# One instruction per tile in place of one per pair of tiles for VectorE's product of gathered rows with silu'd gates

## The reference

```python
dk = jax.nn.silu(edge_attr @ Wdk.T + bdk)
dv = jax.nn.silu(edge_attr @ Wdv.T + bdv)
q_i = q[dst]
k_j = k[src]
v_j = v[src]
attn = jnp.sum(q_i * k_j * dk, axis=1)
attn = jax.nn.silu(attn) * _cosine_cutoff(edge_weight)
msg = v_j * dv * attn[:, None]
agg = jax.ops.segment_sum(msg, dst, num_segments=x.shape[0])
out = agg @ Wo.T + bo
return x + out
```

## Time and profile before

| what | value |
|---|---|
| median of 3 runs | 2825.9 us |
| the profiled execution | 2828.56 us |
| its span, first to last instruction | 2826.3 us |
| PE busy | 2354.1 us (83%) |
| DVE busy | 2156.4 us (76%) |
| POOL busy | 2136.9 us (76%) |
| ACT busy | 1938.9 us (69%) |
| granted TensorE clock, mean | 0.949 |

### The profile page before, as it was taken

One profiled execution on the slowest core, in us unless ns is written; L12 is line 12 of the kernel. 1 busy time (PEld: TensorE's weight loads), 2 busy tenths in 40 slices (PEclk: granted clock), 3 DMA queues, 4 the chain that ended last, 5 costly groups with the idle time before them and its releaser, 6 DMA issues. The chain is left out here.

```text
span 2826.3 us, 52157 instructions
## 1 busy us (share of the span) xinstructions
PE 2354.1 (83%) x12012; PEld 1904.9 (67%) x12012; DVE 2156.4 (76%) x6159; ACT 1938.9 (69%) x4051; POOL 2136.9 (76%) x1792
## 2 busy tenths in 40 slices
PE   7497888888888888888888888888888888888878
PEld 5254676676777676767676776766777767766666
DVE  4586878777878777787777787777777777777776
ACT  3474777777777677777777776777777777767766
POOL 1675878778787788777878778888877778777862
PEclk9799899999999999999999999999999999999999
DMA  8786777877888777788778778778877777778765
GB/s 237 198 215 242 211 234 229 238 234 227 235 236 230 228 224 227 226 234 237 227 231 232 228 234 237 233 229 232 234 231 229 233 231 229 224 234 233 223 188 182
DMA packets 321332, 642.50 MB, mean 227 GB/s; under 512 B 83932, under 2 KB 141648, under 8 KB 321304
## 3 DMA queue, kind: packets, MB, share of 16 engines
q0 software_dynamic: 129840, 418.60, 52.3%
q1 hardware_dynamic: 191464, 223.60, 25.7%
HBM read 583.26 MB, written 58.74 MB: 227 GB/s over the span
## 5 line engine op out<-in xcount | busy, mean ns | idle before, releaser
L949 POOL DMA_INDIRECT e_kv<-kv_tab,e_idx x1568 | 1959.3, 1250 | 495.4 <-issue 453.7
L1153 DVE TENSOR_TENSOR e_gated<-e_kv,e_gate 128x1024 f32<-128x1024 f32 x788 | 954.7, 1221 | 506.5 <-DMA e_kv<-kv_tab,e_idx 504.2
L1081 ACT ACTIVATE e_gate<-e_gate_ps 128x1024 f32<-128x1024 f32 x786 | 780.9, 1020 | 234.2 <-DVE e_gated L1153 217.1
L1097 ACT ACTIVATE weighed_hot<-hot,e_attn 128x128 f32<-128x128 bf16 x1580 | 520.4, 401 | 365.6 <-DVE e_attn L1172 353.9
L1000 PE MATMUL e_sum_ps<-e_gated,weighed_hot 128*128 128x256 f32 x3168 | 750.8, 380 | 3.9 <-ACT weighed_hot L1097 3.9
L1012 PE MATMUL e_gate_ps<-wd_hi_lo,high 128*128 128x512 f32 x1572 | 677.2, 431 | 13.5 <-issue 13.5
L1000 PEld LDWEIGHTS e_sum_ps<-e_gated,weighed_hot 128*128 128x128 f32 x3168 | 603.6, 191 | 101.2 <-ACT weighed_hot L1097 4.7
L1013 PE MATMUL e_gate_ps<-wd_bias,low 128*128 128x512 f32 x1572 | 650.3, 414 | 0.0
L1162 DVE CUSTOM_DVE_ANT_0 e_gated<-e_gated,e_q_ps 128x256 f32<-128x256 f32 x1576 | 573.9, 415 | 0.7 <-PE e_q_ps L1032 0.7
L1031 PE MATMUL e_q_ps<-q_win,hot_t 128*128 128x256 f32 x1572 | 465.1, 323 | 47.7 <-DVE e_dot L1162 47.4
L1020 PE MATMUL e_hot_ps<-ident_bf,hot 128*128 128x128 bf16 x1568 | 160.3, 226 | 315.6 <-DVE hot L1179 315.4
(11 more groups left out here) (156 smaller groups left out, 1398.7 us busy)
## 6 DMA issues: line engine op xcount, KB each, us to landing
e_attr<-attr_groups_dram SPq DMA_DIRECT2D x784, 128.0 KB, 4.6
e_q_next<-q_tab SPq DMA_DIRECT2D x98, 256.0 KB
e_kv<-kv_tab,e_idx POOLq DMA_INDIRECT x1568, 4.5
sum_tab<-e_sums SPq DMA_DIRECT2D x100, 128.0 KB, 4.3
e_prior<-sum_tab SPq DMA_DIRECT2D x99, 128.0 KB
kv_tab<-l_kv_out SPq DMA_DIRECT2D x49, 256.0 KB, 3.5
q_tab<-l_q_out SPq DMA_DIRECT2D x49, 256.0 KB, 3.2
sum_tab<-zeros SPq DMA_DIRECT2D x25, 256.0 KB, 2.9
```

The source lines that it names most:

```text
L949: pool.indirect_dma_start(kv[:, k, :], None, kv_tab, bass.IndirectOffsetOnAxis(ap=idx[:, k:k + 1], axis=0)).then_inc(kv_landed[k // G][k % ...
L1081: nc.scalar.activation(gate[:, 2 * p:2 * p + 2, :], gate_ps[:, 2 * p:2 * p + 2, :], ACT.Silu).then_inc(silu_ready[s][p], 1)
L1097: last = nc.scalar.activation(weighed_hot[:, s % 2, k, :], hot[:, s, :, k], ACT.Copy, scale=attn[:, s * G + k:s * G + k + 1])
L1153: nc.vector.tensor_tensor(gated[:, pair(s, p), :], kv[:, pair(s, p), :], gate[:, 2 * p:2 * p + 2, :], ALU.mult).then_inc(gated_ready[s][p], 1)
```

## The change

`gate_rows` issues one product per tile, 128x512, in place of one per pair, 128x1024. The waits ahead of the first and the signal behind the last stay what they were; between the two stands no wait. A step has 16 such products in place of 8. Nothing else is changed.

```diff
                     dve.wait_ge(kv_landed[s][p], visit.now32 if c >= 2 else visit.late32)
                     dve.wait_ge(silu_ready[s][p], visit.of(c, 2))
-                    nc.vector.tensor_tensor(gated[:, pair(s, p), :], kv[:, pair(s, p), :], gate[:, 2 * p:2 * p + 2, :],
-                                            ALU.mult).then_inc(gated_ready[s][p], 1)
+                    for k in (2 * p, 2 * p + 1):
+                        last = nc.vector.tensor_tensor(gated[:, s * G + k, :], kv[:, s * G + k, :], gate[:, k, :], ALU.mult)
+                    last.then_inc(gated_ready[s][p], 1)
```

## The result

| | median | runs | from, to |
|---|---|---|---|
| before | 2833.47 us | 4 | 2824.22 to 2845.34 |
| changed | 2577.02 us | 4 | 2565.35 to 2578.25 |

The ratio is 0.9084, 95% interval 0.9034 to 0.9133: the changed kernel is 9.2% faster, some 256 us.

A forecast was written before the change was run, and what follows sets the result against it. GpSimd's gathers, delayed by VectorE's products, were taken as the bound. Terms of -86 and +14 us gave -72, from 2828.6 to 2756.6, less 2.7 for the runs' median: 2754 us, range 2670 to 2850.

The forecast's parts named there:

- What bounds the kernel: Edge stage: GpSimd's row of 1568 gathers sets the pace, 25.05 us a step, with 474 us of delays.
- VectorE's extra time costs nothing: Split products add 55 us on VectorE, covered by its 504 us of waiting for rows; chance of its showing 0.05.
- Halves let a plain gather through: A gather meeting just one product goes on at the boundary between its halves; -86 us over 448 gathers.
- The replay: 448 gathers delayed by one product, replayed at their old places against halves: -97, -7 and +18, sum -86 us.
- the slower rival: Halves without a wait block gathers as one product: 47 us slower, 2873 us; 0.20 together with more chained delays.
- The failed step: Gathers kept from an earlier instruction over one or two products stay kept over halves: 86 and 60 gathers, +14 us.
- The chained delays: Gathers arriving as a short instruction gives way to a product without a gap wait it out: 146 gathers, 255 us.
- The 5 in 63: At boundaries between two whole products without a gap, already kept gathers got through 5 times in 63.
- 8 of 8 behind a gap of 0.03 us: Already kept gathers got through 8 of 8 times where 0.03 us or more lay open between whole products.
- The lower bound: Every kept gather is let through at the first half: 86 x 0.61 + 60 x 1.75 = 157 us gained.
- Phases spread: Rival: gathers fall anywhere against VectorE's products, so halves gain 143 us, 2683 us; chance 0.14.
- Phases move: Rival: gathers shift against VectorE, 41 more chained delays swallow the 72 us, 2798 to 2854 us; chance 0.13.

The follow-up runs named there:

- e7: Kernel before with only the second pair of each group (p = 1) split into two products: 2762.7 us, ratio 0.9717.
- e6: Kernel before with only the first pair of each group (p = 0) split into two products: 2672.02 us, ratio 0.9422.
- e18: Kernel before, whole products, with VectorE waiting for its own preceding instruction only ahead of each group's first product: 2608.31 us, ratio 0.922.
- e16: Kernel before, whole products, with VectorE waiting for its own preceding instruction ahead of every product: 2531.29 us, ratio 0.8936.
- e17: Changed kernel (halves) with VectorE waiting for its own preceding instruction only ahead of each group's first product: 2534.74 us, ratio 0.8956.
- e1: Kernel before with the whole product's operands written as one run of 1024 elements: 3199.94 us, ratio 1.0021 (before 3192.31).
- e3: Kernel before with the attention ahead of the attributes' subtraction instead of behind it: 3109.54 us, ratio 0.9745 (before 3192.31).
- e11: Kernel before with three tiny memsets on VectorE ahead of the loop: 3241.8 us, ratio 1.0008 (before 3244.08).
- e12: Changed kernel with three tiny memsets on VectorE ahead of the loop: 3230.93 us, ratio 0.9953 (before 3244.08).
- e10: Changed kernel with an already fulfilled wait ahead of each half: 3311.74 us, ratio 1.0177 (before 3244.08).
- e8: Changed kernel with each tile's product cut once more, four products of 256 columns per pair: 2750.15 us, ratio 0.9689.
- e4: Kernel before without the gates, the product becoming gathered rows times 1.0 with one SBUF input: 3161.98 us, ratio 0.9919.

## Why the prediction was wrong

**What bounds the kernel: right.** In every run where the kernel before took some 2830 us, time follows the gathers' delays nearly one to one: 474 us and a span of 2826 before, 423 and 2778 (e7), 319 and 2663 (e6), 255 and 2601 (e18), 223 and 2574 (changed), 152 and 2529 (e16). The last point has lost a tenth: delays fell by 322 and the span by 297, and of the missing 25 us GpSimd's idle time before its gathers has 23 (518 where it was 495).

**VectorE's extra time costs nothing: right.** The halves take 683 ns, as the subtraction's row had it, and VectorE's busy time in the stage rose from 1923 to 1966 us where 55 were added. Its wait for rows fell to 212 us; 377 had been forecast on the smaller gain, and 504 less 252 less 55 is 197.

**Halves let a plain gather through: right; the size in part by luck.** The replay said 86 us, 94 were measured. But the replay kept every gather at its place and left some 430 of the 448 delayed, and 334 were: others arrive there now. Where a gather met a half in progress with another half right behind it, it went on between the two in 210 of 231 cases; the slower rival, that halves without a wait block as one, is out.

**The failed step: "I take it that they hold such a gather as the whole did: 86 x 0.07 + 60 x 0.14 = +14 us".** The chained delays fell by 197 us. With what was measured the sum comes out: -94 - 197 + 38 (gathers now let in at the ends of the subtraction, the attention and the sums) = -253 against the measured 252. The 5 in 63 on which it rested counted boundaries between two products, for gathers that had been kept already. But the halves do their work one boundary earlier, ahead of the first product: at the end of the attention, where the kernel before kept 75 of 76 and the changed kernel lets in 55 of 70, and at the end of the sums, where the kernel before kept 46 of 57 and the changed kernel lets in 68 of 77. And 8 of 8 behind a gap of 0.03 us, which stood in the same sentence, was the better lead: e16, e17 and e18 are built on it and no gather was kept. The lower bound that the prediction named for this term, 157 us, was called far off; 197 exceed it, since the bound let a gather go at the first half and not ahead of it. (Some 20 us of the 38 that came back are these same places, at the ends of the attention and of the sums; net of them, 177.)

**The rivals.** "Phases spread" had the direction and 143 us, by another road: the plain delays gained little more than the replay. "Phases move" had seen that half of the delay hangs on 0.05 us and that it "could as well lose them", but put no price and no chance on that side.

**What stays open.** Why a product of 512 behind the attention leaves the boundary open when 1024 and 256 don't, with VectorE's instructions at the same distances from the gather, and why 256 delays nobody behind the sums. Neither the operands' form (e1), nor the 4-column instruction (e3), nor the place in the stream (e11, e12), nor an added wait (e10) explains it. That a gap opens it is shown; what happens at a boundary without one is not. Open too is what bounds the groups at 3200 us. There the mean granted TensorE clock was 0.86 to 0.90 in place of 0.94 to 0.98, and GpSimd stood idle 721 to 1272 us before its gathers in place of 490 to 519. 39 to 159 of these waits lasted over 3 us, where the other groups have at most one, and nearly all fell ahead of a gather of even number, where the program waits for VectorE's products. VectorE in turn stood still for up to 10.9 us at a time in e11, against 3.6 in the kernel before. The lower clock goes with it; that it is the cause isn't shown. The same kernels that gain 9 to 11% elsewhere end within 2% of the kernel before.

## What to carry to other kernels

When an instruction on one engine takes several times its median, lay it beside the other engine's timeline and sort it by what ended when it went on: the kinds have different remedies, and the rare long ones can be worth more than the many short ones (here 146 gathers of 1568 held 255 of the 474 us of delays). If GpSimd issues gathers and sets the pace, and VectorE runs instructions with two SBUF inputs back to back, look first for gathers kept over several of them; let VectorE wait for its own last instruction ahead of the first long one (0.21 us four times a step bought 223 us here), and only then cut the long ones. Don't cut for its own sake: halves gained 9%, quarters 3%, and halves on top of the four gaps another 74 us. Such a gain lasts only while the gathers are the bound: with another bound the same change was worth 0.5% (e12).

## What the runs showed of the hardware

- An indirect DMA's issue on GpSimd, which reads its indices from SBUF, waits out a VectorE product with two SBUF inputs that is in progress 0.13 us after its start, for 1.07 us of a 1024-element product or 0.53 us of a 512-element one. SBUF — State Buffer of the Trainium skill, § Who interferes with whom, has the rule (a VectorE instruction with two SBUF inputs contends with a GpSimd instruction that reads SBUF); the trace agrees. The same section says of a probe that tensor_tensor did not stall a DMA; this one, with its indices in SBUF, it does stall. The longest such gather took 1.98 us behind whole products (e18) and 1.47 behind halves (e17).
- A boundary between two VectorE instructions without a gap does not always let a waiting gather in. One was kept 3.1 us in e8, through ten of them; behind a gap of 0.13 us none of 93 was (e16).
- The sums (one input in PSUM, one in SBUF) delayed none of 90 gathers with a gap behind them (e16), kept 46 of 57 with a 1024-element product right behind them (before), held 68 of 77 to their own end with a 512-element one (changed), and delayed none of 21 with a 256-element one (e8).
- The fixed part of this VectorE product between two starts was 0.07 us at 256, 512 and 1024 elements (0.34, 0.60 and 1.14 us from start to start, 1.04 ns an element), against some 0.15 us in the recorded durations (0.42, 0.68 and 1.22 us).
- A float tensor_scalar from SBUF to SBUF took 701 ns for 1024 elements, even when written with a step of two (e4).
